# A directive that places TensorE's instruction blocks in the last stage, with the four call lists laid out anew

## The reference, cut to what matters

```
for i in range(6):
    x = attn_layer(shift_tokens(x), Wqkv[i], q_scale[i], k_scale[i], Wo[i]) + x
    x = ffn_layer(shift_tokens(x), ln_g[i], ln_b[i], W1[i], b1[i], W2[i], b2[i]) + x
# attn_layer: 16 heads of 64; q, k l2-normed and scaled, rotary tables, local attention
# over windows of 32 with one window before, output projection
# ffn_layer: layer norm, W1 to 2 x 341, a * gelu(gate), W2
```

## Time and profile before

| what | value |
|---|---|
| median of 3 runs | 4657.62 us |
| lowest and highest | 4648.66 and 4662.08 us |
| span of the profiled execution | 4655.4 us |
| last stage, from the first to the last of 46 whole pairs of turns | 1540.4 to 4548.8 us, 3008.4 us |
| share of TensorE busy, whole span | 94% |

### The profile page before, as it was taken

The page is one execution under the profiler, slowest core; times in us unless marked ns, Lnnn a source line. Parts: engine busy times, 40 slices in busy tenths (PEclk is TensorE's granted clock), DMA queues, the critical chain, the costliest instruction groups (busy, mean ns, idle before and its releaser), DMA issues.

```text
span 4655.4 us, 137933 instructions
## 1 busy us (share of the span) xinstructions
PE 4360.4 (94%) x56640; PEld 2936.9 (63%) x56640; DVE 3703.2 (80%) x5128; ACT 3238.4 (70%) x6002; POOL 3648.6 (78%) x1951
## 2 busy tenths in 40 slices
PE   7889899978887999999999999999999999999998
PEld 4556688854443666666666666666666666666665
DVE  6874476759997888888888788888888788878885
ACT  4666655657774777777777777777777777777775
POOL 2223344469997999988999899989999898989993
PEclk9999999989998999999999999999999999999999
DMA  2000000023331222322233322323223222322222
GB/s 81 2 2 2 2 1 1 1 110 146 146 146 57 67 63 61 80 65 66 58 70 74 71 63 61 79 66 69 58 67 76 69 64 60 78 68 66 59 68 53
DMA packets 164376, 290.47 MB, mean 62 GB/s; under 512 B 44063, under 2 KB 61350, under 8 KB 159654
## 3 DMA queue, kind: packets, MB, share of 16 engines
q1 hardware_dynamic: 162310, 281.40, 23.2%
q10 hardware_dynamic: 1440, 0.24, 0.0%
HBM read 90.16 MB, written 2.62 MB: 20 GB/s over the span
## 4 chain that ended last, share of the span: by engine, by line
PE 57%; issue 4%; DVE 4%; DMA 2%; ACT 1%; SPq 1%; POOL 0%; DVEq 0%; ACTq 0%
PE ps L2626 19%; PE ps L2682 7%; PE ps L2639 7%; PE ps L2694 7%; PE ps L2655 5%; PE ps L2668 3%; PE ps L2720 3%; PE ps L2736 3%; PE ps L2727 3%; DMA L3f_vw<-L3f_v 2%; DVE L3f_ss L3019 1%; PE ps L2701 1%; PE ps L2707 1%; DVE L3f_raw L3036 1%; SPq L2472 1%
## 5 line engine op out<-in xcount | busy, mean ns | idle before, releaser
L3219 POOL TENSOR_TENSOR L3f_t<-L3f_raw,L3f_rot 128x1024 f32<-128x1024 f32 x384 | 1085.3, 2826 | 246.4 <-DVE L3f_raw L3036 242.8
L2626 PE MATMUL ps<-L3f_wqkv,all_z 128*128 128x512 f32 x2304 | 1154.1, 607 | 11.2 <-DVE L3f_raw L3036 8.8
L3236 POOL TENSOR_TENSOR L3f_raw<-L3f_raw,L3f_t 128x1024 f32<-128x1024 f32 x384 | 911.9, 2375 | 7.5
L3228 POOL TENSOR_TENSOR L3f_raw<-L3f_raw,L3f_rot 128x1024 f32<-128x1024 f32 x384 | 909.0, 2367 | 7.5
L2835 ACT ACTIVATE L3f_sqr<-ps 128x512 f32<-128x512 f32 x768 | 453.1, 595 | 295.8 <-PE ps L2626 292.4
L3036 DVE TENSOR_TENSOR L3f_raw<-ps,L3f_ri 128x512 f32<-128x512 f32 x768 | 498.7, 686 | 163.5 <-ACT L3f_ri L2845 154.4
L3019 DVE TENSOR_REDUCE L3f_ss<-L3f_sqr 128x8 f32<-128x512 f32 x768 | 515.6, 679 | 115.6 <-ACT L3f_sqr L2835 112.3
L2639 PEld LDWEIGHTS ps<-all_ident,L3f_raw 128*128 128x128 f32 x3072 | 363.3, 141 | 307.8 <-issue 270.3
L2626 PEld LDWEIGHTS ps<-L3f_wqkv,all_z 128*128 128x128 f32 x2304 | 395.8, 192 | 234.8 <-issue 180.2
L2639 PE MATMUL ps<-all_ident,L3f_raw 128*128 128x128 f32 x3072 | 474.5, 277 | 9.4 <-POOL L3f_raw L3236 3.7
L2682 PEld LDWEIGHTS ps<-L3f_pT,L3f_vw 128*64 128x64 f32 x12288 | 375.3, 138 | 97.0 <-issue 78.6
(11 more groups left out here) (332 smaller groups left out, 8632.4 us busy)
## 6 DMA issues: line engine op xcount, KB each, us to landing
L3f_vw<-L3f_v SPq DMA_DIRECT2D x1344, 128.0 KB, 2.4
L3a_Bs<-L3a_rows SPq DMA_DIRECT2D x16, 2048.0 KB, 7.1
L3a_Cs<-L3a_rows SPq DMA_DIRECT2D x16, 2048.0 KB, 11.7
L3f_vw<-L3f_v SPq DMA_DIRECT2D x192, 64.0 KB
L3f_wqkv<-in_L_ffn_Wqkv SPq DMA_DIRECT2D x24, 256.0 KB, 4.3
L3f_wqkv<-in_L_ffn_Wqkv SPq DMA_DIRECT2D x6, 512.0 KB, 4.2
L3f_wo<-in_L_ffn_Wo SPq DMA_DIRECT2D x48, 64.0 KB, 2.4
out<-all_x SPq DMA_DIRECT2D x8, 256.0 KB, 3.2
```

Of the source, the lines that this page charges most:

```text
L2626: p.matmul(PS[:, j % 3, :], Z[:, u % NSEQ, t * P:t * P + P], w, start=True, stop=True).then_inc(proj.sem)
L3219: g.tensor_tensor(t.rearrange("p h (b e) -> p h b e", b=2), r.rearrange("p h (b e) -> p h b e", b=2)[:, :, ::-1, :], w[:, 1, :].rearrange( ...
L3228: g.tensor_tensor(r, r, w[:, 0, :].unsqueeze(1).broadcast_to((P, H, HD)), ALU.mult).then_inc(cosined.sem)
L3236: g.tensor_tensor(r, r, t, ALU.add).then_inc(rotated.sem)
```

## The change

The four lists hold the same calls as before, in another order; some calls of a list move over its end into the next turn (`gelu` 0 and 1, `exponent(., 1)`, `value(., "v1a")`, `below(., 1)`, `share(., 0)`, and the places of GpSimd's steps). Counted through the new list, the eight boundaries fall inside the four `scores` (at 67, 124, 137 and 182 of 257 instructions), inside three `values` (23, 88 and 89 of 129) and at the start of `ffn_up(., 0)`.

```diff
+        FETCHED, BEGIN = 256, 104
...
+            def aligned(u):
+                if not 0 <= u < N:
+                    return
+                p.addr_align(FETCHED, offset=BEGIN)
...
+            scores(2 * i + 2, 0)
             turn_qk(2 * i + 2, 1, 0)
-            scores(2 * i + 2, 0)
             project(2 * i + 3, "v0b")
...
+            scores(2 * i + 2, 1)
             turn_p(2 * i + 1, 1)
-            scores(2 * i + 2, 1)
...
             variance(2 * i + 1)
-            project(2 * i + 4, "v0a")
             scores(2 * i + 3, 0)
             turn_qk(2 * i + 3, 1, 1)
             turn_p(2 * i + 2, 0)
+            project(2 * i + 4, "v0a")
+            turn_qk(2 * i + 3, 1, 2)
...
             ffn_gate(2 * i + 1, 0)
             ffn_gate(2 * i + 1, 1)
+            ffn_gate(2 * i + 1, 2)
             project_out(2 * i + 2)
+            ffn_up(2 * i + 1, 0)
             project(2 * i + 4, "v1b")
-            ffn_gate(2 * i + 1, 2)
+            ffn_up(2 * i + 1, 1)
             project(2 * i + 5, "q0a")
-            ffn_up(2 * i + 1, 0)
-            ffn_up(2 * i + 1, 1)
             ffn_up(2 * i + 1, 2)
             centre(2 * i + 2)
+            aligned(2 * i + 2)
             project(2 * i + 5, "q0b")
...
             length(2 * i + 2, "k1")
-            gelu(2 * i - 1, 0)
-            gelu(2 * i - 1, 1)
-            squared(2 * i + 3, "q0a")
+            value(2 * i + 2, "v1a")
             gelu(2 * i - 1, 2)
             value(2 * i + 2, "v1b")
+            exponent(2 * i + 1, 1)
             centred(2 * i)
+            squared(2 * i + 3, "q0a")
...
             turned(2 * i + 3, 0, 0)
-            length(2 * i + 3, "k1")
             spread(2 * i + 1, 1)
-            affine(2 * i)
-            value(2 * i + 3, "v1a")
+            value(2 * i + 3, "v1b")
             turned(2 * i + 3, 0, 1)
             squared(2 * i + 4, "q0a")
+            affine(2 * i)
             output(2 * i + 1, 1)
             squared(2 * i + 4, "q0b")
             exponent(2 * i + 2, 1)
-            value(2 * i + 3, "v1b")
...
             squared(2 * i + 4, "k1a")
+            output(2 * i + 2, 1)
+            gelu(2 * i + 1, 0)
             squared(2 * i + 4, "k1b")
-            value(2 * i + 4, "v1a")
-            output(2 * i + 2, 1)
-            exponent(2 * i + 3, 1)
+            gelu(2 * i + 1, 1)
...
             norm(2 * i + 2, "q0a")
+            norm(2 * i + 2, "q0b")
             residual(2 * i - 1)
-            norm(2 * i + 2, "q0b")
             scale(2 * i, 0)
             sums(2 * i + 2, "k0a")
             sums(2 * i + 2, "k0b")
             bounded(2 * i + 2, "k0")
+            share(2 * i, 1)
             normal(2 * i - 1)
...
+            norm(2 * i + 2, "k1a")
             share(2 * i + 1, 0)
-            norm(2 * i + 2, "k1a")
             norm(2 * i + 2, "k1b")
             scale(2 * i + 1, 0)
-            total(2 * i + 1, 1)
             residual(2 * i)
...
             bounded(2 * i + 3, "q0")
+            total(2 * i + 1, 1)
+            normal(2 * i)
+            sums(2 * i + 3, "k0a")
             norm(2 * i + 3, "q0a")
             norm(2 * i + 3, "q0b")
-            sums(2 * i + 3, "k0a")
-            normal(2 * i)
...
```

More of the change, by code:

```diff
@@ L2753, in turn_back @@
                     mm.then_inc(z_turned.sem)
+            scores(2 * i + 2, 0)
             turn_qk(2 * i + 2, 1, 0)
-            scores(2 * i + 2, 0)
             project(2 * i + 3, "v0b")
             project(2 * i + 3, "q1a")
+            turn_qk(2 * i + 2, 1, 1)
             project(2 * i + 3, "q1b")
-            turn_qk(2 * i + 2, 1, 1)
             project(2 * i + 3, "k1a")
@@ L2786, in pe @@
             turn_p(2 * i + 2, 0)
+            project(2 * i + 4, "v0a")
+            turn_qk(2 * i + 3, 1, 2)
             project(2 * i + 4, "v0b")
             project(2 * i + 4, "q1a")
-            turn_qk(2 * i + 3, 1, 2)
             values(2 * i + 2, 0)
             project(2 * i + 4, "q1b")
+            project(2 * i + 4, "k1a")
             turn_qk(2 * i + 3, 1, 3)
@@ L2794, in pe @@
             scores(2 * i + 3, 1)
-            project(2 * i + 4, "k1a")
             project(2 * i + 4, "k1b")
+            values(2 * i + 2, 1)
             project(2 * i + 4, "v1a")
-            values(2 * i + 2, 1)
             ffn_gate(2 * i + 1, 0)
             ffn_gate(2 * i + 1, 1)
+            ffn_gate(2 * i + 1, 2)
             project_out(2 * i + 2)
+            ffn_up(2 * i + 1, 0)
             project(2 * i + 4, "v1b")
-            ffn_gate(2 * i + 1, 2)
+            ffn_up(2 * i + 1, 1)
             project(2 * i + 5, "q0a")
-            ffn_up(2 * i + 1, 0)
-            ffn_up(2 * i + 1, 1)
             ffn_up(2 * i + 1, 2)
             centre(2 * i + 2)
+            aligned(2 * i + 2)
             project(2 * i + 5, "q0b")
@@ L2939, in act @@
             length(2 * i + 2, "k1")
-            gelu(2 * i - 1, 0)
-            gelu(2 * i - 1, 1)
-            squared(2 * i + 3, "q0a")
+            value(2 * i + 2, "v1a")
             gelu(2 * i - 1, 2)
             value(2 * i + 2, "v1b")
+            exponent(2 * i + 1, 1)
             centred(2 * i)
+            squared(2 * i + 3, "q0a")
             squared(2 * i + 3, "q0b")
             turned(2 * i + 2, 0, 0)
+            root(2 * i)
             length(2 * i + 3, "q0")
@@ L2950, in act @@
             turned(2 * i + 2, 0, 1)
-            root(2 * i)
             turned(2 * i + 2, 0, 2)
@@ L2955, in act @@
             length(2 * i + 3, "k0")
+            value(2 * i + 3, "v0a")
             spread(2 * i + 1, 0)
-            value(2 * i + 3, "v0a")
             turned(2 * i + 2, 1, 0)
@@ L2960, in act @@
             squared(2 * i + 3, "q1a")
+            turned(2 * i + 2, 1, 1)
             squared(2 * i + 3, "q1b")
-            turned(2 * i + 2, 1, 1)
+            squared(2 * i + 3, "k1a")
             length(2 * i + 3, "q1")
             turned(2 * i + 2, 1, 2)
-            squared(2 * i + 3, "k1a")
             output(2 * i + 1, 0)
@@ L2969, in act @@
             exponent(2 * i + 2, 0)
+            length(2 * i + 3, "k1")
+            value(2 * i + 3, "v1a")
             turned(2 * i + 3, 0, 0)
-            length(2 * i + 3, "k1")
             spread(2 * i + 1, 1)
-            affine(2 * i)
-            value(2 * i + 3, "v1a")
+            value(2 * i + 3, "v1b")
             turned(2 * i + 3, 0, 1)
             squared(2 * i + 4, "q0a")
+            affine(2 * i)
             output(2 * i + 1, 1)
@@ L2988, in act @@
             root(2 * i + 1)
+            affine(2 * i + 1)
             length(2 * i + 4, "k0")
-            value(2 * i + 4, "v0a")
             turned(2 * i + 3, 1, 1)
             spread(2 * i + 2, 0)
-            turned(2 * i + 3, 1, 2)
+            value(2 * i + 4, "v0a")
             squared(2 * i + 4, "q1a")
             value(2 * i + 4, "v0b")
+            turned(2 * i + 3, 1, 2)
             output(2 * i + 2, 0)
@@ L2998, in act @@
             turned(2 * i + 3, 1, 3)
-            affine(2 * i + 1)
             length(2 * i + 4, "q1")
@@ L3125, in dve @@
             sums(2 * i + 2, "q0a")
+            below(2 * i, 1)
             sums(2 * i + 2, "q0b")
-            share(2 * i, 0)
             bounded(2 * i + 2, "q0")
@@ L3136, in dve @@
             bounded(2 * i + 2, "k0")
+            share(2 * i, 1)
             normal(2 * i - 1)
-            share(2 * i, 1)
+            hidden(2 * i + 1, 0)
             norm(2 * i + 2, "k0a")
             norm(2 * i + 2, "k0b")
-            hidden(2 * i + 1, 0)
+            top(2 * i + 1, 0)
+            below(2 * i + 1, 0)
             scale(2 * i, 1)
-            top(2 * i + 1, 0)
             sums(2 * i + 2, "q1a")
-            below(2 * i + 1, 0)
             sums(2 * i + 2, "q1b")
@@ L3178, in dve @@
             norm(2 * i + 3, "k0a")
+            share(2 * i + 1, 1)
             norm(2 * i + 3, "k0b")
@@ L3183, in dve @@
             sums(2 * i + 3, "q1b")
-            share(2 * i + 1, 1)
             bounded(2 * i + 3, "q1")
@@ L3192, in dve @@
             bounded(2 * i + 3, "k1")
+            total(2 * i + 2, 0)
             norm(2 * i + 3, "k1a")
@@ L3195, in dve @@
             hidden(2 * i + 2, 1)
+            share(2 * i + 2, 0)
             top(2 * i + 2, 1)
-            total(2 * i + 2, 0)
-            below(2 * i + 2, 1)
         def pool(i):
@@ L3236, in add @@
                 g.tensor_tensor(r, r, t, ALU.add).then_inc(rotated.sem)
-            cosine(2 * i, "q1")
+            add(2 * i, "k0")
             sine(2 * i, "k1")
+            cosine(2 * i, "k1")
             add(2 * i, "q1")
-            cosine(2 * i, "k1")
+            add(2 * i, "k1")
             sine(2 * i + 1, "q0")
-            add(2 * i, "k1")
             cosine(2 * i + 1, "q0")
@@ L3250, in pool @@
             cosine(2 * i + 1, "q1")
+            sine(2 * i + 1, "k1")
             add(2 * i + 1, "q1")
-            sine(2 * i + 1, "k1")
             cosine(2 * i + 1, "k1")
@@ L3255, in pool @@
             sine(2 * i + 2, "q0")
+            sine(2 * i + 2, "k0")
```

(5 more changed lines are left out.)

## The result

The changed kernel takes 4902.12 us (median; 4898.59 to 4905.45), the kernel before 4659.85 us: 1.0526 times as long, 95% interval 1.051 to 1.0542. The forecast of 4634 us, its range to 4748 us and its sign were wrong; the third rival, pads that bind, is what happened, at a dearer price than its 51 ns.

The account below looks back on a forecast made before the run. The prediction took the last stage to be bound by TensorE's own work. Its terms, -33 - 23 + 29 + 0 + 3 = -24 us, took the median of 4657.6 us to 4634 us, with a range of 4592 to 4748 us.

Parts of the forecast that it names:

- third rival: Ahead of `project` q0b, pads at 51 ns each outlast the array's queued work: +110 us, 4744 us; chance 0.30.
- Part 4: TensorE's 79 pads a pair behind `centre`: 17 ns each, 1.3 us a pair, hidden but for 0.2 us: 0.
- Part 1: TensorE's instruction block boundaries, now fixed: the issue stalls inside `scores` go, -33 us, bounds 0 and -37.
- fourth rival: At TensorE's block boundaries: they aren't the cause of the stalls, or don't stay placed; 4667 us, chance 0.10.
- Part 2: TensorE's wait for the load of Wo: its transfers start 3.1 us earlier, -23 us, bounds -12 and -25.
- Part 3: Seam of ScalarE's list: three table loads delay `residual`, v1b and `turn_qk`, 0.6 us a pair, +29 us, bounds 0 and +60.
- Part 5: `turn_p(2i + 2, 0)` waiting for `normal`, which `scale` delays: 0.3 us a pair, +3 us, between -11 and +30.
- first rival: Two table loads or none at ScalarE's seam, and `scale` between GpSimd's steps: -67 us, 4591 us; chance 0.16.
- Part 6: Remaining waits: `residual` ahead of `centre` stays, 11.4 us; `scores` trades places with `turn_qk` or `turn_p` without a wait.

## Why the prediction was wrong, and where it was right

**Part 4, the pads, is the step that failed.** It took 17 ns a pad, ScalarE's price of a semaphore found set, hence 1.3 us a pair and 0 in the sum. A pad takes 75 ns. The frame around the number held: the pads began when `residual` ended, and 1.6 us of the array's work, `ffn_up` and `centre`, lay beside them (I had said 1.1). The argument for the low price, that "a pad asks for nothing", was no row of the trace. The nearest row by kind was TensorE's own semaphore instruction, 51 ns, "and up to twice that from one to the next". It is the time from one to the next that counts: the NOP itself is on record with 13 ns, and 73 ns apart. The Trainium skill (PSUM — Partial Sum Buffer, Engine vs sequencer instructions) has a nop executed on the sequencer like a semaphore operation. These records agree: the pads pass on the sequencer while the array works off its matmuls. The third rival, which priced a pad by TensorE's own semaphore instruction, was the right case, though its 51 ns was too low as well.

I had also priced the gap only by its length. The third rival at 75 ns would be 5.9 us of pads less 1.1, about 4.8 us a pair, 230 us; measured are 309 (289 in the 46 pairs, 20 at the two ends). Between the change and the same kernel with its pads spread, by the starts of successive calls (mean of 44 pairs), q0b comes 4.4 us later behind `centre`, and the five calls from q0b on take 2.2 us longer: that is the lower clock behind each gap, for which the earlier trace rows had a row. The rest are the longer rows of pads at the two ends, 183 and 133, where I counted with 79 everywhere.

**Part 1, fixed boundaries: -33.** Right in its cause and nearly in size: 4605.0 to 4568.6 us, -36, with the pads hidden; -50 with the long rows at the two ends gone too. The issue waits that went were 35 us. The cause is shown twice over by the same number of pads a pair with boundaries 128 places on: +147 and +177 us. That speaks against the fourth rival: in these runs a multiple of 256 instructions costs up to 2.8 us where the block before passed quickly. The Trainium skill (Runtime: NRT & Kernel Launch, Instruction fetch mechanics) has such a crossing "mostly hidden". By their count that holds here: wandering boundaries gave 24 stalls in `scores` at 354 boundaries, and even the ill chosen ones gave 139 in `scores` and `values` at 8 x 46 = 368. By their cost it doesn't: those 139 are 137 us.

**Part 2, Wo: -23.** Moving v1b alone gave -17, its interval from -10 to -23; the wait fell from 17.6 to 2.1 us.

**Part 3, the seam: +29.** Three loads came, at the places named. Their price is 24.8 (known to some 12 us) and 24.7 us in two pairs of kernels. `residual` came late, much as forecast: from its end to q0b it is 3.98 us before and 1.43 in the new order without the directive (medians), where I had 1.0 (2717.4 to 2718.4). But the place of the loss was off. Of the 0.61 us a pair between the kernels with spread pads, with and without the loads (starts of successive calls, mean of 44 pairs), 0.29 lie at `turn_p(2i + 1, 1)` and 0.33 at `ffn_up` 0, v1b and the first `scores`, not at q0b and `turn_qk`.

**Part 5, turn_p: +3.** It was a gain: the row of 10.6 us is absent. `scale` takes 1.4 us in the changed kernel and 1.7 with the pads spread (median), 3.3 before, so it fits between GpSimd's steps, as the first rival had it.

**Part 6, the rest: 0.** Not quite. The kernel before to that without directive and extra loads is -52 us, of which Wo and `turn_p` explain some 26. In a quiet pair several calls follow one another more closely: in the medians from start to start, `project` v0b and k1a of the odd unit took 0.96 and 0.99 us before and take 0.86 in the new order, and one `scores` 1.50 and now 1.41. These three are 0.3 us a pair, some 15 us. Which exchange of places does it wasn't tried, and the other 11 us, about what the time of that kernel is uncertain by, stay open.

So with its pads hidden the change goes from 4658.6 to 4593.3 us, a gain of 65 us where I had forecast 24. That this is near the first rival's 4591 is chance: that rival had two loads or none, and here there were three; the gain of part 6 was in no sum.

## What to carry to other kernels

A pad for alignment is a real instruction: count all of them, first pair included, at 75 ns each on TensorE's sequencer, from the last wait ahead of them, against the array's work that is then queued (with all 79 behind `project_out` that was 4.3 us). Put in small groups, or behind a call of many long matmuls, they cost nothing here. Where to start the blocks matters as much as that they are fixed: the wrong start cost more here than wandering boundaries.

An instruction's own duration in a trace is not its price. Take the time from one to the next, and when the nearest row of the same engine and another engine's row disagree, take the engine's own.

## What the runs showed of the hardware that was not expected

- NOPs of TensorE last 13 ns on record and follow each other every 73 to 75 ns; rows of 29 to 183 lie within 0.15 us of one line.
- The array's queue held 17 matmuls ahead of the one running, 4.3 us of work, while the sequencer worked on pads. At that place the pads began 1.6 us after the last wait was met, at the start of a matmul, as if the queue had been full until then.
- Behind a gap of 4.2 us in TensorE's work the granted clock was 0.58 in the mean of the next 7.1 us; one of 1.5 us lengthened the next two matmuls by 0.08 us only.
- A fixed bad start of the blocks gave two stalls in nearly every pair, 137 us in `scores` and `values`, against 33 us in `scores` for wandering ones.
